# A two-block transformer on one core: split projections in its second cross attention, batches overlapped in its first, and a third tile in its normalisations

## The reference, cut to what matters

```
# first cross attention (linear), per batch; feature map of q and of k
f = (relu(y) + 1e-6) / softplus(scale)
f = f**3 * |f| / |f**3|                      # the norms over the 256 features
kv, ksum = k^T v, sum of k   (per head);   out = q kv / (q ksum + 1e-6)

# second cross attention (softmax), per batch, 16 heads of 64
q, k, v = x Wq, ctx Wk, ctx Wv               # 256 -> 1024 features each
out = softmax(q k^T / 8 + mask) v Wo^T + bo
```

## Time and profile before

| | |
|---|---|
| median of 3 runs | 3266.99 us (3266.16 to 3267.48) |
| the profiled execution | 3266.41 us, of it 3264.6 us from the first to the last instruction |
| TensorE busy / weight loads busy | 2818.9 us (86%) / 2049.9 us (63%) |
| VectorE / ScalarE / GpSimd busy | 1942.7 (60%) / 1693.0 (52%) / 694.7 us (21%) |
| mean granted TensorE clock | 0.911 of full speed |
| stages from first to last (start, us) | a0 10.5, x0 959, f0 1168, a1 1724, x1 2442, f1 2891 |

### The profile page before, as it was taken

The page is one execution under the profiler, slowest core; times in us unless marked ns, Lnnn a source line. Parts: engine busy times, 40 slices in busy tenths (PEclk is TensorE's granted clock), DMA queues, the critical chain, the costliest instruction groups (busy, mean ns, idle before and its releaser), DMA issues. The chain is left out here.

```text
span 3264.6 us, 49578 instructions
## 1 busy us (share of the span) xinstructions
PE 2818.9 (86%) x16640; PEld 2049.9 (63%) x16640; DVE 1942.7 (60%) x4248; ACT 1693.0 (52%) x3120; POOL 694.7 (21%) x806
## 2 busy tenths in 40 slices
PE   6788888888855559999997999999989999949998
PEld 3344444444334436766765888888886777738887
DVE  4778777877754346556644566565664454444444
ACT  3887888788842224444443555555555555542221
POOL 1122222222110004444451000000003565620000
PEclk9889988998776669999998999999998999979999
DMA  2000000000000020110012000000001000020000
GB/s 98 4 4 4 0 3 3 3 0 3 1 17 26 25 67 23 28 40 22 23 22 57 1 1 1 1 1 1 1 26 64 7 3 6 4 88 7 6 6 29
DMA packets 87121, 59.37 MB, mean 18 GB/s; under 512 B 54688, under 2 KB 76576, under 8 KB 86496
## 3 DMA queue, kind: packets, MB, share of 16 engines
q1 hardware_dynamic: 87008, 57.89, 5.9%
HBM read 41.10 MB, written 8.39 MB: 15 GB/s over the span
## 5 line engine op out<-in xcount | busy, mean ns | idle before, releaser
L1820 POOL TENSOR_SCALAR x_weights<-x_weights,x_sums 128x256 f32<-128x256 f32 x256 | 231.7, 923 | 884.0 <-DVE x_sums L1857 884.0
L670 DVE SCALAR_TENSOR_TENSOR a_w<-a_w,a_sinks 128x384 f32<-128x384 f32 x512 | 332.8, 715 | 31.5 <-ACT a_w L505 31.5
L1074 POOL TENSOR_SCALAR f_weights<-f_weights,f_sums 128x256 f32<-128x256 f32 x256 | 232.1, 924 | 271.5 <-DVE f_sums L1304 271.5
L484 ACT ACTIVATE a_e<-psum 128x1024 f32<-128x1024 f32 x192 | 195.3, 1017 | 158.0 <-PE psum L343 118.7
L1506 ACT ACTIVATE a_turned_w_hi<-psum 128x512 fp32r<-128x512 f32 x256 | 139.0, 595 | 195.2 <-PE psum L1440 195.1
L1232 ACT ACTIVATE f_weights<-psum,f_negmax 128x256 f32<-128x256 f32 x256 | 117.8, 472 | 215.5 <-DVE f_negmax L1298 215.5
L685 DVE SCALAR_TENSOR_TENSOR a_w<-a_e,psum 128x512 f32<-128x512 f32 x256 | 162.8, 677 | 96.1 <-ACT a_e L486 86.5
L340 PE MATMUL psum<-a_qT,a_kT_half 32*128 32x512 f32 x512 | 166.3, 729 | 60.6 <-DVE a_w L685 48.8
L1570 DVE TENSOR_REDUCE a_negmax<-psum 128x1 f32<-128x1024 f32 x128 | 156.7, 1224 | 89.8 <-PE psum L123 89.8
L486 ACT ACTIVATE a_e<-a_e 128x1024 f32<-128x1024 f32 x192 | 202.9, 1057 | 6.1
L1790 ACT ACTIVATE x_weights<-x_masked_s,x_negmax 128x256 f32<-128x256 f32 x256 | 126.9, 496 | 146.4 <-DVE x_negmax L1853 146.3
(11 more groups left out here) (305 smaller groups left out, 7092.7 us busy)
## 6 DMA issues: line engine op xcount, KB each, us to landing
x_ctxT<-in_x_ctxT SPq DMA_DIRECT2D x16, 256.0 KB, 2.7
f_xnT<-all_xnT_all SPq DMA_DIRECT2D x16, 256.0 KB, 2.3
f_pv_rows<-f_pv SPq DMA_DIRECT2D x8, 512.0 KB, 3.1
f_pv_groups<-f_pv_rows SPq DMA_DIRECT2D x8, 512.0 KB
f_w<-in_f_w SPq DMA_DIRECT2D x2, 2048.0 KB, 10.1
all_x_all<-in_x SPq DMA_DIRECT2D x1, 2048.0 KB, 8.9
a_wq<-in_a_wq SPq DMA_DIRECT2D x2, 1024.0 KB, 9.4
a_wo<-in_a_wo SPq DMA_DIRECT2D x2, 1024.0 KB, 12.2
```

Of the source, the lines that this page charges most:

```text
L484: act.activation(e[:, x, :], psS[x], ACT.Exp).then_inc(exp_done, 1)
L670: ins = dve.scalar_tensor_tensor(part, part, sinks[:, col:col + 1], part, ALU.is_ge, ALU.mult)
L1074: ins = pool.tensor_scalar(w, w, sums[:, k, h, t:t + 1], None, ALU.mult)
L1820: ins = pool.tensor_scalar(w, w, sums[:, k, h, t:t + 1], None, ALU.mult)
```

## The change

Three edits. In `normalise` the ring has three tiles and the loop is written out over 16 tiles. In `linear_attention` every engine runs `over_batches`: PE projects batch b+1 ahead of the rest of batch b, DVE finishes b-1 in between; the four scalings by the factor move from DVE to ACT, the copy of `qT` from ACT to DVE, the addition to `x_all` from DVE to POOL; max, +1e-6 and the scale become one instruction, as 1e-6 is put into the biases once. In `cross_attention1` the projections and the output product use `split_product` on high and low parts: weights are cut once at the start, x and the context once per batch, `oT` in every pair; the context comes per batch from DRAM and is no longer loaded whole; all bodies are written out (`each_batch`).

```diff
-        self.normalised, self.transposed, self.copied = (s.sems(n, TT) for n in ("normalised", "transposed", "copied"))
+        self.normalised, self.transposed, self.copied = (s.sems(n, LN_RING) for n in ("normalised", "transposed", "copied"))
...
+            for t in range(TILES):
+                r, again = t % LN_RING, t // LN_RING
+
+                wait(dve, transposed[r], before[r] + again)
+                dve.tensor_scalar(xn[:, r, :], x_all[:, t, :], rstd[:, t:t + 1], shift[:, t:t + 1],
+                                  ALU.mult, ALU.add).then_inc(normalised[r], 1)
...
+            def project(b):
                 pe.wait_ge(x_here, b * 16 + 16)
                 pe.wait_ge(ctx_here, b * 16 + 16)
 
-                pe.wait_ge(out_taken, b)
+                wait(pe, features_raw, b)
...
+                    if n == 2:
+                        wait(pe, v_taken, b)
...
+            def body(b, new, ahead, old):
+                if ahead:
+                    project(b + 1)
+                if new:
+                    pe.wait_ge(k_scaled, b + 1)
+                    pe.wait_ge(v_taken, b + 1)
+
+                    wait(pe, kv_ready, b)
...
+                    ins.then_inc(kv_summed, 1)
+                    pe.wait_ge(q_scaled, b + 1)
+
+                    wait(pe, qT_ready, b)
...
+                    ins.then_inc(q_turned, 1)
+                    pe.wait_ge(kv_ready, b + 1)
+                    pe.wait_ge(qT_ready, b + 1)
+
+                    wait(pe, o_made, b)
...
+            def body(b, new, ahead, old):
+                if new:
+                    act.wait_ge(squared, b + 1)
+                    act.wait_ge(cubed, b + 1)
+                    for i in range(2 * TT):
+                        ins = act.activation(f2[:, i, :], f3[:, i, :], ACT.Square, accum_out=norm6[:, i:i + 1])
+                    ins.then_inc(sixth, 1)
+                    act.wait_ge(ratio_ready, b + 1)
+                    act.activation(factor[:], factor[:], ACT.Sqrt).then_inc(factor_ready, 1)
+                    act.wait_ge(factor_ready, b + 1)
+                    for i, done in ((TT, None), (TT + 1, k_scaled), (0, None), (1, q_scaled)):
+                        ins = act.activation(f3[:, i, :], f3[:, i, :], ACT.Copy, scale=factor[:, i:i + 1])
...
+                if ahead:
+                    act.wait_ge(features_raw, b + 2)
+                    for i in range(2 * TT):
+                        ins = act.activation(f2[:, i, :], f[:, i, :], ACT.Square, accum_out=norm2[:, i:i + 1])
+                    ins.then_inc(squared, 1)
...
+                    pool.tensor_tensor(x_b, x_b, o[:], ALU.add).then_inc(x_added, 1)
...
+            def body(b, new, ahead, old):
+                if new:
+                    dve.wait_ge(squared, b + 1)
+                    wait(dve, q_turned, b)
+                    dve.tensor_tensor(f3[:], f2[:], f[:], ALU.mult).then_inc(cubed, 1)
+                if old:
+
+                    dve.wait_ge(out_ready, b)
...
+                if ahead:
+
+                    wait(dve, cubed, b + 1)
+                    dve.wait_ge(projected, b * 3 + 4)
+                    dve.tensor_tensor(f[:, TT:2 * TT, :], tile(0), bias(bk), ALU.add).then_inc(raw_f, 1)
+                if new:
+                    dve.wait_ge(sixth, b + 1)
+                    dve.reciprocal(factor[:], norm6[:]).then_inc(inverted, 1)
+                    dve.wait_ge(inverted, b + 1)
+                    dve.tensor_tensor(factor[:], factor[:], norm2[:], ALU.mult).then_inc(ratio_ready, 1)
+                if ahead:
+                    dve.wait_ge(projected, b * 3 + 5)
+                    dve.tensor_tensor(f[:, 0:TT, :], tile(1), bias(bq), ALU.add).then_inc(raw_f, 1)
+                    dve.wait_ge(raw_f, b * 2 + 4)
+                    dve.scalar_tensor_tensor(f[:], f[:], FOCUS_EPS, inv_scale[:].unsqueeze(1).to_broadcast([P, 2 * TT, D]),
+                                             ALU.max, ALU.mult).then_inc(features_raw, 1)
+                if new:
+                    dve.wait_ge(kv_summed, b + 1)
+
+                    wait(dve, out_ready, b)
...
+                    dve.wait_ge(q_turned, b + 1)
+                    dve.tensor_copy(qT[:], psum[:, 4, :].rearrange("p (c t) -> p c t", c=CC)).then_inc(qT_ready, 1)
+                if ahead:
+                    dve.wait_ge(projected, b * 3 + 6)
...
+                    ins.then_inc(v_taken, 1)
...
+def each_batch(eng, body):
+
+    for b in range(-1, B + 1):
+        body(b, 0 <= b < B, b + 1 < B, b >= 1)
...
-            with sp.Fori(0, B) as b:
-
-                sp.wait_ge(v_ready, b * V)
-                sp.dma_start(ctxT[:], a["ctxT"][bass.ds(b * D, D), :].rearrange("(k p) n -> p k n", p=P))\
+            for b in range(B):
+                if b >= 1:
+                    sp.wait_ge(ctx_low, b)
+                sp.dma_start(ctx_raw[:], a["ctxT"][b * D:(b + 1) * D, :].rearrange("(k p) n -> p k n", p=P))\
                   .then_inc(ctx_here, 16)
...
+                    if i % 2:
+                        pe.wait_ge(w_low, 2)
+                        pe.wait_ge(ctx_low, bb + 1)
+                    else:
+                        pe.wait_ge(w_low, 1)
+                        pe.wait_ge(x_low, bb + 1)
...
-                            ins = pe.matmul(qk_bank(i)[:, j * T:(j + 1) * T], (wq, wk)[i % 2][:, c, lo:lo + P], src,
-                                            start=(c == 0), stop=(c == CC - 1))
+                            ins = split_product(pe, qk_bank(i)[:, j * T:(j + 1) * T], [z[:, c, lo:lo + P] for z in (wq, wk)[i % 2]],
+                                                [z[:, bb % 2, c, :] for z in ctxT] if i % 2 else [z[:, c, :] for z in xT], c == 0, c == CC - 1)
...
+            def weights_high(w, n):
+                act.activation(w[0][:], raw[n], ACT.Copy).then_inc(w_high, 1)
+
+            def x_split(bb):
+
+                wait(act, qk_ready, (bb - 1) * QK + 7)
+                act.activation(xT[0][:], xnT_all[:, bb], ACT.Copy).then_inc(x_high, 1)
+
+            def ctx_split(bb):
+                act.wait_ge(ctx_here, bb * 16 + 16)
+                wait(act, v_ready, (bb - 1) * V)
+                act.activation(ctxT[0][:, bb % 2], ctx_raw[:], ACT.Copy).then_inc(ctx_high, 1)
...
+                    if b == -1 and p == 0:
+                        weights_high(wq, 0)
+                    if b == -1 and p == 1:
+                        weights_high(wk, 1)
+                    if b == -1 and p in (3, 4):
+                        weights_high(wv if p == 3 else wo, p - 1)
+                    if ahead and p == 0:
+                        ctx_split(b + 1)
+                    if ahead and p == 1:
+                        x_split(b + 1)
...
-                        dve.tensor_copy(oT[:, k, :], psum[:, O0, 0:T]).then_inc(oT_ready, 1)
-
-            over_batches(dve, body)
+                        dve.tensor_copy(oT[0][:, k, :], psum[:, O0, 0:T]).then_inc(oT_high, 1)
+                        dve.wait_ge(oT_high, n + 1)
+                        dve.tensor_tensor(oT[1][:, k, :], psum[:, O0, 0:T], oT[0][:, k, :].bitcast(F32), ALU.subtract)\
+                           .then_inc(oT_ready, 1)
+
+            each_batch(dve, body)
```

More of the change, by code:

```diff
@@ L139, in normalise @@
         norm.runs += 1
-        b0 = run * B
+        before = [run * len(range(r, TILES, LN_RING)) for r in range(LN_RING)]
         s = Scope(nc, stack, f"ln{run}")
@@ L194, in _ @@
             act.activation(std[:], mean_var[:, :, 1], ACT.Sqrt, bias=eps[:, 0:1]).then_inc(std_ready, 1)
-            with act.Fori(0, B) as b:
-                for t in range(TT):
-                    act.wait_ge(transposed[t], b0 + b + 1)
-                    act.activation(xnT_all[:, bass.ds(b, 1), :, t * P:(t + 1) * P], psT[:, t, 0:CC, :],
-                                   ACT.Copy).then_inc(copied[t], 1)
+            for t in range(TILES):
+                r, again = t % LN_RING, t // LN_RING
+                act.wait_ge(transposed[r], before[r] + again + 1)
+                act.activation(xnT_all[:, t // TT, :, t % TT * P:(t % TT + 1) * P], psT[:, r],
+                               ACT.Copy).then_inc(copied[r], 1)
 BR, NH, DH = 4, 16, 16
@@ L772, in _ @@
                     ins.then_inc(projected, 1)
-                pe.wait_ge(features, b + 1)
-                for c in range(CC):
-                    for t in range(TT):
-                        ins = pe.matmul(psum[:, 3, c * (P + 1):(c + 1) * (P + 1)], f3[:, TT + t, c * P:(c + 1) * P],
-                                        v1[:, t, c, :], start=(t == 0), stop=(t == TT - 1))
-                ins.then_inc(kv_summed, 1)
-                for c in range(CC):
-                    for t in range(TT):
-                        ins = pe.transpose(psum[:, 4, c * T + t * P:c * T + (t + 1) * P], f3[:, t, c * P:(c + 1) * P],
-                                           ident[:])
@@ L817, in _ @@
+            over_batches(act, body)
+        @block.gpsimd
+        def _(pool):
```

(21 more changed lines are left out.)

202 lines of the change are left out of this document (95 added, 107 removed).

## The result

The changed kernel takes **3159.47 us** (median of 4 runs, 3154.44 to 3169.87) beside 3267.23 us for the kernel before on the same chip: a ratio of 0.9674, 95% interval 0.9654 to 0.9695. That is 108 us less where 141 were forecast: 3126 was the forecast, 3102 to 3176 its range. The profiled execution is the fastest of the four, 3154.44 us with a span of 3152.6, against 3266.41 before.

A forecast was written before the change was run, and what follows sets the result against it. Linear attention bound by a chain, second cross attention by PE, normalisation by a ring of two. Terms -95.7, -28 and -19, less 1.7 for early low clock, give -141; 3266.4 - 141 + 0.6 = 3126 us, range 3102 to 3176.

The forecast's parts named there:

- Rival 1: Linear attention: loops interleave badly or PE stays at the low clock, 15 us a batch; +38, 3164 us; chance 0.17.
- Rival 2: Second cross attention: POOL becomes late, its 1.96 us margin overrun by 0.5 a pair; +32, 3158 us; chance 0.10.
- Linear attention: Overlapped batches at 9.7 us each bring the main block from 187.8 to 92.1 us: -95.7.
- (a): Linear attention's load loop: `xnT` and `ctxT` keep one buffer each, closing over a batch in 8.9 us.
- (b): Linear attention's loop through PE's order: projections, k^T v, mask and qT copy on DVE, output; 8.8 us a batch.
- for meetings: Linear attention: three loops that nearly tie lose some at each meeting, so 9.7 us a batch was taken.
- Split passes: Second cross attention: three cheaper passes per product save 5.4 of 51.5 us a batch, less 0.4; times 8, -40.
- rival 3: Second cross attention: weight loads show in the split passes, 0.19 us more per 256-column pass; +219, 3345 us; chance 0.02.
- DVE comes to some 30 of 46 us, ACT to 29: covered.: Second cross attention: work added to DVE and ACT lies beside PE; 0.4 us a batch allowed, bounds 0 and 2.
- Start of the second cross attention: PE waits for cut weights; first scores near 24 us into the block against 12.1: +11.5, bounds +6 and +16.
- Normalisation: Three tiles in the ring: 0.48 us a tile against 0.75; -19 over the stages, bounds -10 and -25.
- Not loading 2 MB of context lies under the normalisation and gives nothing: Second cross attention's loads: 4.4 MB instead of 6.4, hidden under the normalisation, so no gain.

The follow-up runs named there:

- experiment 9: The changed kernel with two load buffers for x and context in the linear attention, PE's and SP's bodies written out; 3153.59 us (one run).
- experiment 2: The changed kernel with ACT's high parts of the q/k units placed ahead of the pair's exponentials; 3124.23 us, ratio 0.9564 to the kernel before.
- experiment 7: The changed kernel with two tiles instead of three in the normalisations, loop still written out; 3173.28 us, ratio 0.9712 to the kernel before.
- experiment 3: The changed kernel with the second cross attention of the kernel before in full; 3152.49 us, ratio 0.9652 to the kernel before.
- experiment 5: The changed kernel with DVE writing the high part of `oT` twice in every pair; 3192.24 us, ratio 0.9767 to the kernel before.
- experiment 4: The changed kernel with the second cross attention's output product back in plain f32, `oT` copied once per pair; 3150.08 us, ratio 0.9633 to the kernel before.

## Why the prediction was right, and where it was wrong

Between the profiled executions it forecast -141 us and got -112. The total lies in the range, but not because the terms were right. The second cross attention missed by 43.5 us, the stages around it gave 14 us more than forecast, and the range's upper end, 3176, was there for rivals 1 and 2, neither of which occurred in a filled batch. That it also covered this loss was luck. By its own steps:

- **Linear attention: right.** -95.7 less 1.7 for filling were forecast for the main block, and it fell by 94.4 (100.4 less 6.0 of normalisation). The loops, by name: (a) the loads were put at 8.9 us a batch and held it at 9.1 to 9.2; (b) PE's order was put at 8.8, and the batch is 8.6 once the loads are out of the way (experiment 9). I took 9.7 "for meetings": the filled batches were better than that, the first two worse (10.6 and 12.2 us between k units), and the two errors cancelled. The clock over the block was 0.88, not above 0.9. Right by its sum more than by its terms.
- **Split passes: the price was right.** 46.7 us of PE work a batch after the ring is cut, 46.81 from output unit to output unit, against 51.53: 4.72 us a batch, forecast 5.0. The v units came out dearer than put: two of them take 2.87 us, not 2.72. The passes stand 0.12 us apart, each with its own weight load of 0.19 us, so rival 3 did not occur. The Trainium skill ("TensorE: Matmul & The Clock Gate", section "The mechanism", not the one that the prediction names) says that a weight load overlaps running matmuls only when it goes to other rows of the array; these full-height passes, 0.12 us apart, disagree.
- **The step that failed: "DVE comes to some 30 of 46 us, ACT to 29: covered."** The sums were right (29.2 and 28.9) and the conclusion did not follow. The second `oT` step stands in a ring over two in-order engines, 6.28 us long in a pair with two units, and PE needs 5.86 us for such a pair since the change. Its place was even named ("behind the second `oT` step queue the next pair's mask and maximum"), but the margin that I checked was POOL's. The ring cost 37.6 us of the stage (experiment 2): 25.6 in the five filled batches, 7.0 ahead of the first output unit and 4.9 in the last two batches. A filled batch lost 3.05 us at its output units and 1.25 in two shorter waits, and two of the five another 1.5 with the lower clock. I had allowed 0.4 us a batch and a bound of 2; it was 4.5 to 6.
- **Start of the second cross attention: mis-sized.** +13.6 us to the first scores (26.5 against 12.9) where +11.5 were forecast. The mechanism was as described: cuts of `wv` and `wo` ahead of the low parts of units 2 and 3.
- **What was left even without the ring's loss.** With the ring cut the main block is 20.5 us shorter than before, where 28 were forecast. The five filled batches save 23.6 us and the end of the stage 4.5, the start costs 7.6. In the last batch, with no projections beside it, PE waits 2.78 and 3.78 us for POOL (2.87 and 3.10 before), so the cheaper passes help little there; the forecast counted all eight batches alike.
- **Normalisation: the term was mis-sized.** 0.40 us a tile where 0.48 were taken, because the written-out loop itself saves 2.5 us (experiment 7). From the root to the first product of the main block the five stages other than x1 gained 2.2, 6.0, 5.7, 1.0 and 5.8 us between these two executions, in sum 20.6 where 14.8 were forecast. The first stage, for which I had put nothing, gave 2.2 of them; a1, for which I had put 2.5, gave 1.0, as its loads keep PE waiting 5.7 us. The rest of the 28.7 us in the table is not the normalisations' and came with this execution: a0 moved between -0.6 and -5.7 over the executions with the same code.
- **"Not loading 2 MB of context lies under the normalisation and gives nothing": wrong by up to 7 us**, in the direction of a hidden gain. With the short normalisation the old loads are 7 us late (experiment 3), so what the normalisation gained in this stage exists only because of the smaller loads.
- **Rival 1** (PE stays slow in x0, 3164) gave nearly the measured time for a reason that did not occur. **Rival 2** (POOL late) did not occur in the filled batches either: it was right that engines beside PE become late there, wrong in which.

## What to carry to other kernels

When PE's work per step shrinks, don't compare the busy sums of the other engines with the new step alone; follow each ring of hand-overs over in-order engines once round and compare its length, waits included. Where a ring is too long, look for work that waits in it without needing to: one reordering on ACT was worth 35 us here, three times what this part of the change had lost without it. And a shorter prologue is worth only as much as the loads beneath it allow.

## What was not expected of the hardware

- A wait of some 3 us in an otherwise full stretch can cost more than itself: in two of the five filled batches between 2430 and 2690 us the clock fell to 1.2 GHz behind it (batch mean 0.97), once at the first pass (0.55 us instead of 0.36) and once a little later, and the batch took 1.5 us more. Behind waits above 4 us every output unit of experiment 5 began at 1.2 GHz. Even behind 1.68 us two batches of experiment 4 were 1.7 us longer.
- Writing out a short loop over three engines took DVE's wait for a slot from 0.65 to 0.39 us a round, with the same number of slots (experiment 7). What in the loop costs it was not tried.
- Stages with the same code in the same order moved by up to 9 us between executions of these kernels (a0's main block 934.8 to 939.5 us, a1 from root to root 708.9 to 717.8), so a single total cannot price a part; the stage's own length could, to 0.3 us in the linear attention.
